# All engine loops written out, and two spreads of the routing weights loaded from the route stage

## What is computed

```
x += 0.5 * moe(layernorm(x))          # 64 experts, 8 chosen per token, and one shared expert
x += head_attention(layernorm(x))     # 16 heads of 8, no projections before, one after
x += 0.5 * moe(layernorm(x))          # the same weights again
x += 0.5 * gated_cell(layernorm(x))   # a recurrence over the 4 batches, then tanh
x += decayed_attention_and_mlp(layernorm(x))
x += 0.5 * gated_cell(layernorm(x))
```

```
affinity = sigmoid(h @ router_w)                       # token x 64
top 8 of them, divided by their sum -> router_mask     # token x 64, zero for the others
shared = (silu(h @ sg) * (h @ su)) @ sd
routed = sum over e of (silu(h @ gate[e]) * (h @ up[e]) * router_mask[:, e]) @ down[e]
```

## Time and profile before

| | |
|---|---|
| median of three runs | 3015.69 us |
| profiled execution | 3016.72 us, span 3014.9 us |
| PE busy | 2673.9 us (89%) |
| DVE busy | 2308.4 us (77%) |
| ACT busy | 1804.5 us (60%) |
| POOL busy | 965.2 us (32%) |
| code fetched by DMA | 1.15 MB (70 packets) and 0.76 MB (94 packets) |

### The profile page before, as it was taken

The page is one execution under the profiler, slowest core; times in us unless marked ns, Lnnn a source line. Parts: engine busy times, 40 slices in busy tenths (PEclk is TensorE's granted clock), DMA queues, the critical chain, the costliest instruction groups (busy, mean ns, idle before and its releaser), DMA issues. The chain is left out here.

```text
span 3014.9 us, 37679 instructions
## 1 busy us (share of the span) xinstructions
PE 2673.9 (89%) x11635; PEld 2163.0 (72%) x11635; DVE 2308.4 (77%) x3342; ACT 1804.5 (60%) x2927; POOL 965.2 (32%) x761
## 2 busy tenths in 40 slices
PE   7799999988999999999999978999999884555678
PEld 5688777866888888888888756887878663344456
DVE  6677777867999999999999776777877547776555
ACT  3355554547888888888888634555545443443365
POOL 2466666650000000000000034666666403444310
PEclk8899999998999999999999988999999886777788
DMA  1566655632111111111111106665656000000000
GB/s 55 128 142 132 152 123 122 146 99 76 44 52 53 50 46 53 53 45 51 53 53 43 46 25 144 132 151 126 147 128 140 21 22 28 14 14 0 8 7 28
DMA packets 76820, 222.76 MB, mean 74 GB/s; under 512 B 12145, under 2 KB 16881, under 8 KB 76529
## 3 DMA queue, kind: packets, MB, share of 16 engines
q1 hardware_dynamic: 76432, 220.77, 29.7%
q10 hardware_dynamic: 224, 0.07, 0.0%
HBM read 205.87 MB, written 10.75 MB: 72 GB/s over the span
## 5 line engine op out<-in xcount | busy, mean ns | idle before, releaser
L629 POOL TENSOR_TENSOR moe_experts_lo<-moe_experts_hidden,moe_experts_hi 128x512 fp32r<-128x512 f32 x512 | 662.3, 1294 | 388.3 <-ACT moe_experts_hi L567 388.3
L873 DVE TENSOR_TENSOR heads_e_lo<-heads_e,heads_e_hi 128x1024 fp32r<-128x1024 f32 x512 | 624.4, 1220 | 75.3 <-ACT heads_e_hi L822 66.4
L817 ACT ACTIVATE heads_e<-psum 128x1024 f32<-128x1024 f32 x512 | 525.0, 1025 | 131.2 <-PE psum L766 131.1
L574 ACT ACTIVATE psum<-psum 128x512 f32<-128x512 f32 x512 | 298.0, 582 | 493.6 <-PE psum L94 493.6
L601 DVE TENSOR_TENSOR moe_experts_weighted<-moe_experts_spread,psum 128x512 f32<-128x512 f32 x512 | 351.3, 686 | 238.2 <-PE psum L94 181.2
L92 PE MATMUL psum<-moe_n_hi,moe_w_lo 128*128 128x512 f32 x1024 | 406.2, 397 | 38.0 <-DVE moe_experts_hidden L606 34.2
L93 PE MATMUL psum<-moe_n_lo,moe_w_hi 128*128 128x512 f32 x1024 | 404.5, 395 | 0.0
L94 PE MATMUL psum<-moe_n_hi,moe_w_hi 128*128 128x512 f32 x1024 | 403.9, 394 | 0.0
L92 PE MATMUL psum<-heads_e_hi,heads_v_lo 128*128 128x512 f32 x1024 | 400.5, 391 | 0.7 <-DVE heads_u L841 0.7
L94 PE MATMUL psum<-heads_e_hi,heads_v_hi 128*128 128x512 f32 x1024 | 399.5, 390 | 0.0
L93 PE MATMUL psum<-heads_e_lo,heads_v_hi 128*128 128x512 f32 x1024 | 399.1, 390 | 0.0
(11 more groups left out here) (426 smaller groups left out, 4527.2 us busy)
## 6 DMA issues: line engine op xcount, KB each, us to landing
moe_experts_spread<-moe_mask SPq DMA_DIRECT2D x128, 1024.0 KB, 11.5
heads_scale<-heads_inverse_copy SPq DMA_DIRECT2D x64, 512.0 KB, 3.7
heads_left<-heads_parts SPq DMA_DIRECT2D x128, 64.0 KB
heads_right<-heads_parts SPq DMA_DIRECT2D x128, 64.0 KB
moe_experts_raw<-in_gate SPq DMA_DIRECT2D x16, 256.0 KB, 12.0
moe_experts_raw<-in_up SPq DMA_DIRECT2D x16, 256.0 KB
moe_experts_raw<-in_down SPq DMA_DIRECT2D x16, 256.0 KB
heads_parts<-heads_e_hi SPq DMA_DIRECT2D x16, 256.0 KB, 3.2
```

Source lines behind the costliest of these rows:

```text
L574: act.activation(psum[:, GATE + p % 2, :], psum[:, GATE + p % 2, :], ACT.Silu).then_inc(silu_ready, 1)
L629: pool.tensor_tensor(lo[:, p, :], hidden[:, p % 2, :], f(hi[:, p, :]), ALU.subtract).then_inc(low_ready, 1)
L817: act.activation(e[:, s % 4, :], wide, ACT.Exp, scale=HEAD ** -0.5, accum_out=sums[:, h % 2, s:s + 1]).then_inc(exp_done, 1)
L873: dve.tensor_tensor(e_lo[:, s, :], e[:, s % 4, :], f(e_hi[:, s, :]), ALU.subtract).then_inc(low, 1)
```

## The change

First, every `Fori` becomes an ordinary Python loop, so the whole program is straight code, with constants where registers were. Second, the tile `spread` and its two semaphores are allocated in `moe_layer`, ahead of the layernorm; the function that loads a body's spread is handed to both stages. In the route stage, SP issues the spread of body 0 (tokens of chunks 0 and 1) behind the store of chunk 2, and that of body 1 (chunks 2 and 3) behind the store of chunk 4, each once the stores that it reads have landed. In `experts` SP begins with body 2.

The core of the diff:

```diff
-def each_chunk(eng, step):
-
-    step(0, 0, False)
-    step(1, 1, False)
-    with eng.Fori(1, CHUNKS // 2 - 1) as r:
-        for j in range(2):
-            step(r * 2 + j, j, False)
-    step(CHUNKS - 2, 0, False)
-    step(CHUNKS - 1, 1, True)
+def each_chunk(step):
+
+    for c in range(CHUNKS):
+        step(c, c % 2, c == CHUNKS - 1)
...
                     sp.dma_start(mask_dram[:, c * BANK:(c + 1) * BANK], mask[:, c % 2, :]).then_inc(mask_stored[c % 2], 16)
+                    if c in (2, 4):
+                        for stored in mask_stored:
+                            sp.wait_ge(stored, 8 * c)
+                        spread_body(sp, c // 2 - 1)
...
             two_groups(0)
-            with eng.Fori(1, GROUPS // 2) as k:
+            for k in range(1, GROUPS // 2):
                 two_groups(k)
...
-                load_spread(0)
                 for body in range(GROUPS * BODIES):
-                    if body + 1 < GROUPS * BODIES:
-                        load_spread(body + 1)
+                    if 2 <= body + 1 < GROUPS * BODIES:
+                        sp.wait_ge(weighted_ready, body * 2 * GROUP)
+                        spread_body(sp, body + 1)
...
+        spread = sb(f"{tag}_spread", [P, 2, GROUP, 2 * BANK])
+        sem = sems_in(ctx, nc, f"{tag}_spread")
+        spread_loaded = [sem("loaded_even"), sem("loaded_odd")]
...
-                with pe.Fori(0, BATCH - 1) as t:
+                for t in range(0, BATCH - 1):
                     from_cell(t)
                     from_input(t + 1)
```

More of the change, by code:

```diff
@@ L288, in _, with route_and_share @@
                             take_low(pool, "pool", c)
-def route_and_share(nc, tag, psum, consts, router, weights, n_hi, n_lo, mask_dram, x):
+def route_and_share(nc, tag, psum, consts, router, weights, n_hi, n_lo, mask_dram, x, spread_body):
     identity = consts["identity"]
@@ L424, in leave @@
                     dve.wait_ge(routed_turned, c + 1)
[L425 to L428, removed]
+                    after(dve, mask_stored[j], 16 * (c // 2))
                     dve.tensor_copy(mask[:, j, :], psum[0:EXPERTS, MASK, :]).then_inc(mask_ready, 1)
@@ L455, in step, with experts @@
                     pool.tensor_tensor(lo[:, j, :], hidden[:, j, :], f(hi[:, j, :]), ALU.subtract).then_inc(low_ready, 1)
-                each_chunk(pool, step)
-def experts(nc, tag, psum, consts, dram, w_hi, w_lo, n_hi, n_lo, mask_dram, x):
+                each_chunk(step)
+def experts(nc, tag, psum, consts, dram, w_hi, w_lo, n_hi, n_lo, x, spread, spread_loaded, spread_body):
     gate_dram, up_dram, down_dram = dram
     PER = CHUNKS * GROUP
-    BODIES = CHUNKS // 2
     GATE, UP, DOWN = 0, 2, 6
@@ L650, in moe_layer, with spread_body @@
         w_lo = sb(f"{tag}_w_lo", [P, 2, PARTS, COLS], F32R)
+        spread = sb(f"{tag}_spread", [P, 2, GROUP, 2 * BANK])
+        sem = sems_in(ctx, nc, f"{tag}_spread")
+        spread_loaded = [sem("loaded_even"), sem("loaded_odd")]
+        by_expert = mask_dram.rearrange("(g p i) t -> i g p t", i=2, p=GROUP)
+        def spread_body(eng, body):
+            group, tokens = body // BODIES, slice(body % BODIES * 2 * BANK, (body % BODIES + 1) * 2 * BANK)
+            for i in range(2):
+                eng.dma_start(spread[i * HIDDEN:(i + 1) * HIDDEN, body % 2, :, :],
+                              by_expert[i, group, :, tokens].unsqueeze(0).to_broadcast([HIDDEN, GROUP, 2 * BANK])
+                              ).then_inc(spread_loaded[body % 2], 16)
         with ExitStack() as small:
@@ L658, in moe_layer @@
             route_and_share(nc, f"{tag}_route", psum, consts, parts["router"], [parts[name] for name in names[1:]],
-                            n_hi, n_lo, mask_dram, x)
+                            n_hi, n_lo, mask_dram, x, spread_body)
         experts(nc, f"{tag}_experts", psum, consts, [dram[name] for name in ("gate", "up", "down")],
-                w_hi, w_lo, n_hi, n_lo, mask_dram, x)
+                w_hi, w_lo, n_hi, n_lo, x, spread, spread_loaded, spread_body)
 def head_attention(nc, tag, psum, consts, dram, x):
@@ L962, in _ @@
                     act.copy(c_hi[:, half, :], cell[:, half, :]).then_inc(high_ready, 1)
-                with act.Fori(0, BATCH) as t:
+                for t in range(0, BATCH):
                     for half in range(HALVES):
@@ L983, in _ @@
                     dve.tensor_tensor(c_lo[:, half, :], cell[:, half, :], f(c_hi[:, half, :]), ALU.subtract).then_inc(low_ready, 1)
-                with dve.Fori(0, BATCH) as t:
+                for t in range(0, BATCH):
                     for half in range(HALVES):
@@ L1069, in rows @@
             prepare(0)
-            with eng.Fori(0, BATCH - 1) as b:
+            for b in range(0, BATCH - 1):
                 attend(b)
@@ L1082, in _ @@
                 load(0)
-                with sp.Fori(1, BATCH) as b:
+                for b in range(1, BATCH):
                     wait_apart(sp, products["v"], b, sp_passed)
@@ L1321, in _ @@
             def _(pool):
-                with pool.Fori(0, BATCH) as b:
+                for b in range(0, BATCH):
                     def sum_rotated(name, factor):
```

16 lines of the change are left out of this document (7 added, 9 removed).

## The result

| | before | after |
|---|---|---|
| median | 3015.16 us (4 runs, 3014.28 to 3017.92) | 2971.84 us (4 runs, 2970.51 to 2974.20) |
| ratio | | 0.9856, interval 0.9839 to 0.9873 |
| profiled execution | 3016.72 us, span 3014.9 | 2974.20 us, span 2972.4 |

Forecast was 2969, range 2962 to 2979. The two profiled executions differ by 42.5 us; the sum had said 46.8.

What follows compares the result with a forecast made beforehand. PE was taken to set the pace, losing time behind DVE's jumps and at the experts' start. Terms -27.2 - 21.0 + 1.0 + 1.1 - 0.2 - 0.5 = -46.8 took 3016.72 to 2969.9; predicted 2969 us, range 2962 to 2979.

Steps and rivals of the forecast that it cites:

- Term A: Experts: writing out the loops removes four jumps back, behind which DVE waits for code; -27.2 us, bounds 0 and -27.2.
- rivals 1 and 5: Experts: straight code still comes late, for DVE (2996 us, chance 0.05) or for PE (3055 us, chance 0.03).
- Rival 5: Experts: PE waits 4.5 us at each of some 19 code pages, +86 us, 3055; chance 0.03.
- Term B: Start of the experts: the first two spreads come early, gaining 10.5 us a layer, 21.0 in both.
- Rival 3: Start of the experts: something else holds the first body, so early spreads gain nothing; 2990 us, chance 0.04.
- Term C: Route stage: stores sit behind the early spreads on SP's queue; +0.5 us a layer, +1.0 in both.
- rival 2: Route stage: a spread takes 3 us longer and delays the last store; +3 a layer, 2975 us, chance 0.12.
- Term D: End of each experts layer: one more semaphore clearing with a barrier; 0.55 us each, +1.1 in both layers.
- Term E: Other loops written out: gated cell -0.2 us from fewer table loads, MLP -0.5 from less register work.

Runs made afterwards that it cites:

- Loops only: Every loop of the kernel before written out, spreads left at the head of the experts; 2987.41 us, ratio 0.9904.
- DVE only: Kernel before with only DVE's loop in the experts written out, all other loops kept; 2982.72 us, ratio 0.9889.
- the measurement of jumps: Kernel before plus a stage of test loops of varied length per engine; DVE's jump cost 0.5 us over 160 instructions, 3.0 over 320.
- Spreads only: Kernel before with all loops kept, only the spreads of bodies 0 and 1 begun in the route stage; 2994.08 us, ratio 0.9924.
- one clearing: Changed kernel with the spread's two semaphores cleared with the experts' own, one barrier less per layer; 2967.56 us, ratio 0.9847.
- DVE and spreads: Kernel before with DVE's experts loop written out and the first two spreads begun in the route stage; 2969.91 us, ratio 0.9859.

## Why the prediction was right, by its steps

**Term A (-27.2): right, and shown.** Loops only gave 27.2. The hit to the tenth is luck: "DVE only" takes the same stalls away, 27.5 us by the matmuls' pace, and gave 31.9. The reason given (DVE waits for code behind a jump, PE behind DVE, then PE pays at the lower clock) is shown by "DVE only" and by the measurement of jumps. The Trainium skill (Runtime: NRT & Kernel Launch, Instruction fetch mechanics) has engines hold two blocks, 512 instructions in all, PE 2048, and says that a jump out of the blocks held stalls. The runs agree in kind: up to 288 instructions no stall on DVE, ACT or POOL, at 640 one on each, and none on PE with 640 matmul rows. They don't give 512 as the limit: DVE stalls by 3.0 us at 320, where ACT doesn't, and ACT by 2.6 at 384. Straight code came in time: rivals 1 and 5 fall, with 8 and 9 code packets in 246 us and no idle PE. (Rival 5's price counted the 19 pages of one layer; for both layers it is 38, so that 4.5 us each would have been 171 us and 1.2 us a page would have undone the gain.)

**Term B (-21.0): right.** Spreads only gave 20.6. Per layer the excess of the first 144 matmuls over 0.2268 us each fell from 13.59 to 2.54 and from 13.49 to 2.99: 11.05 and 10.5 against 10.5. Rival 3 falls; nothing stood long behind the spread.

**Term C (+1.0): right in size, 0.75 + 0.0.** Its steps were a little short: store 3 took 8.3 us (estimate 7), copy 7 came 2.4 us later than its time, not 1.5, and so the last store went out 0.8 us later than assumed (91.58, of which 1.9 is what the first norm had taken longer, against 88.9). Only DVE's slack kept rival 2 away.

**Term D (+1.1): the barrier is nearly right, its part in the total isn't shown.** PE's first matmul of the next norm comes 0.8 and 0.7 later than before, and taking the clearing out gave 0.4 and 0.7 back, against 0.55. No median of either kernel can tell one barrier from none.

**Term E (-0.7): its parts have the right sign, and the clock took them back.** The cell's table loads are 2 and not 8, and the first pass of each cell is 0.1 us shorter (8.25 becomes 8.16). The MLP, from its first to its last gate row, is 1.1 us shorter (48.7 becomes 47.6; -0.5 was forecast). But from there to the last norm it takes 2.2 us more (10.2 becomes 12.4). The rows before and after:

```profile
2921.20:2931.50 10.30, 5.56 (x20) 3.50 (x19) 5.32 (x9) 1.35 (x3) 0.00 (x0) 0.96 0.03 8
2877.60:2890.00 12.40, 7.65 (x20) 4.89 (x19) 5.29 (x9) 1.26 (x3) 0.25 (x1) 0.77 0.04 13
```

The same 20 matmuls at a mean clock of 0.77 and not 0.96. All six profiles with the MLP's loops written out have 12.3 to 12.4 us there, all six with the loops kept 10.2 to 10.7; the norm and cell behind it are 1.0 shorter, and the sum of the three is 142.4 before and 142.5 after. So here the lower clock came with the edit and wasn't chance; what ties it to the edit stays open.

**What the sum left out** is the clock in the norms and the decayed attention. In the profiled pair the changed kernel had +1.7 in the first norm, +0.7 in the head attention's, +1.9 in the cell's and +0.6 in the decayed attention with the MLP's norm: 4.9 us of losses that no term named, against the 4.3 by which the sum was too good. For the 3 us between 2969 and the median 2971.84 they are the likely reason, as far as one profile of each can tell. The range had room for them; that the median came as near as 3 us to a sum without them is partly luck.

## What to carry to other kernels

A jump back over a long body costs, one over a short body hardly: here 0.5 us with its wait up to 288 instructions, and about 3 us with idle DMA engines, 3.5 to 5.7 with busy ones and often a second gap, from 320 (DVE) or 384 (ACT). Write out the loop of the engine that the bottleneck waits for; with that done, writing out the others won nothing here that could be told. Load what a stage needs first while the stage before runs, but count what its bytes hold up on the same queue. Where PE waits for others all the time, a stage's length moves by 2 to 3 us with the clock, so don't add up terms under a microsecond there, and don't believe an edit that wins 3 us in such a place until the reverse edit loses them.

## What the runs showed of the hardware that was not expected

- One norm, the same code and nothing different ahead of it, took 25.5 to 25.8 us in some profiles and 27.1 to 27.7 in others; in three slower ones (changed, one clearing, DVE only) the clock granted in 24 to 40 us was 0.50, in two faster ones (before, DVE and spreads) 0.56 and 0.57.
- The passes of the decayed attention alternate between about 76.2 and 77.5 us in seven of twelve profiles, in either order (before 77.5, 76.3, 77.7; after 76.2, 77.5, 76.1); in the other five all are between 76.0 and 76.8.
- A code packet on q14 is 8 KB and on q8 16 KB (0.74 MB in 90 packets, 1.51 MB in 92); written out, the kernel fetches 0.34 MB more, more on q8 (0.36) and less on q14 (0.02), and no wait for it shows.
- TensorE too stalls at a jump: 3.6 to 3.9 us with 1280 matmul rows in the body, none with 640, nor with the 576 of the experts.
- The same loop of the experts has a second gap of 4.8 to 5.0 us at both jumps of layer 0 and none over 2.2 at those of layer 1.
